# Sixteen key and value pieces of layer 1 moved from the convolution's stage into layer 0's cross attention, and routing counts in bf16

## The chip, the cores and the metric

The kernel runs on one core of a Trainium2 chip. The metric is the device time of one execution in microseconds. Engines: PE is the matrix engine, PEld its weight loads, DVE the vector engine, ACT the scalar engine, POOL GpSimd, SP the queue that issues most transfers. A `q` behind an engine's name is its sequencer.

## The reference

A decoder of two layers over x of 32 x 128 x 256 (32 tiles of 128 rows), all f32. Each of six stages is followed by a residual sum and a layer norm:

```python
x = ln(x + L0_attn(x))                      # 16 heads, correlation scores
x = ln(x + L0_xattn(x, ctx, ctx))           # 16 heads of 16, |i - j| <= 64
x = ln(x + L0_ffn(x))                       # rms norm, 8 bit rounding, one matmul
x = ln(x + L1_attn(x))                      # long convolution (EMA), gated attention
x = ln(x + L1_xattn(x, ctx, ctx))           # 16 heads of 64
x = ln(x + L1_ffn(x))                       # 8 experts, top 2, capacity, gelu
# L1_xattn begins with, for every tile of ctx:
k = ctx @ Wk.T + bk; v = ctx @ Wv.T + bv    # 256 -> 1024 each
# L1_ffn: pos = cumsum(onehot(top_i)) over the 4096 rows, keep = pos < capacity
```

Layer 1's keys and values depend on ctx alone, so they can be made at any time before layer 1's cross attention.

## The kernel before

**Keys and values in pieces.** `EarlyKeysValues` (L1248) makes them ahead, for 16 groups of two tiles, 8 pieces a group, 128 pieces in all: four of keys (two banks' halves, each with its bias on ACT) and four of values. `make` puts the matmuls of a piece on PE, `keep` its copy on ACT; PSUM banks alternate (`self.ps[n % 2]`), and `make` of piece n waits until piece n - 2 is kept. ACT also issues the stores to DRAM (keys of a group when its first value piece is kept, values when the next group's first key piece is kept, 1 MB each) and the load of the context of the group after next. `load_weights` brings 1 MB of key weights, the bias and 1 MB of value weights; the contexts of groups 0 and 1 are loaded behind them on SP. The first piece waits for the key weights, the bias and the first context.

**Where the pieces go.** Before: 4 at the end of layer 0's cross attention, 66 in the feed-forward stage (9 + 8 x 6 + 9), 58 in the convolution's stage: 20 ahead of the convolution (`CONV_FIRST`), one behind each of its 16 steps, 22 after it.

**Layer 0's cross attention** (`l0_xattn`, L794) works on 8 groups of 4 tiles. Every engine walks the same list of steps s in its own written order (`walk`, L866), each entry (lag, count, function) acting on tile s - lag. Per tile: PE makes the scores; DVE takes their maximum, subtracts it (`shift`, in two halves), later sums the exponentials (`sums`); ACT makes the exponentials; POOL scales them; PE transposes them (`transpose_e`, four parts), two steps later, multiplies by the values (`apply`), and one step later by the output weights (`multiply`); DVE adds the residual. `transpose_e` of a tile's second part waits for the residual, as they share a bank. Per group, in the four steps before its first tile: the transposes of x (part 0), the projections of q (part 1), k (part 2) and v (part 3), all through the two banks `ps_p`, which the early pieces share. ACT copies each of them out (`copy_xt`, `bias_q`, `bias_k`, `copy_v`). The step of part 0 is the step in which a group's first tile is scored (s % 4 = 0). On SP, `load(g)` brings x and the context of a group; the context's buffer is free when the values of group g - 2 are projected, and SP issues in order.

**The feed-forward stage** (`l0_ffn`) puts its pieces by number after `L0X_LAST`.

**The convolution's stage** (`mega_conv`, L1664): SP issues four loads of the normalised x in runs of 256 bytes, then the weights of the gated attention. PE makes the first pieces, waits for the input, then runs 16 steps of the convolution with a piece behind each, then the rest. When ACT has written the last step's result, SP issues four stores of it, also in runs of 256 bytes, waits for them and issues the first loads of it for the gated attention. The next stage begins when all engines are done, ACT's stores too.

**Layer 1's cross attention** (`l1_xattn`, L2123) counts rows per expert in groups of two tiles: `count` multiplies `hot` (128 x 32, zeros and ones) once by a triangle of ones (`upto`) and once by ones, both f32; DVE adds up the counts.

## Time and profile before

| what | us |
|---|---|
| runs of the kernel before | 2377.5, 2382.82, 2383.73; median 2382.82 |
| profiled execution, its own time | 2379.42 |
| its span in the trace | 2377.7 |
| PE busy | 2168.2 (91%) |
| DVE busy | 1329.3 (56%) |
| ACT busy | 1111.6 (47%) |
| POOL busy | 923.3 (39%) |
| mean granted PE clock, share of full speed | 0.967 |

The stages follow one another: layer 0's attention to about 404 us, its cross attention to 726, the feed-forward stage to 871, the convolution's stage 872 to 1005, the gated attention to about 1305, layer 1's cross attention to 1817, the experts to the end. A share over the whole span mixes these, so the windows and timelines by stage say more. Busy of PE includes the latency of the last matmul of a run, so a PE that is shown busy all the time can still hold gaps of a tenth of a microsecond.

### The profile page before, as it was taken

The page shows a single profiled execution, that of the slowest core. Times are in us where ns is not written, and L with a number is a line of the kernel's source. Part 1 is how long each engine was busy: PE and PEld are TensorE (multiplying, and loading weights), DVE is VectorE, ACT ScalarE, POOL GpSimd, SP SyncE. Part 2 cuts the span into 40 slices and gives each one's busy share as a digit, 9 for nine tenths or more (in the row PEclk, how much of TensorE's full clock was granted, in tenths as well). Part 3 has the DMA queues.
Part 4 walks back from the last instruction along what each step waited for, and adds up shares of the span by engine and source line. Part 5 has one row for each costly group of instructions (what it writes and reads, how often), then busy time and mean ns, then how long its engine had stood idle before and what let it go on. Part 6 is the DMA issues. An engine that isn't in the chain of part 4 may idle for free. (4 is left out here: it accounts for less than half of the span.)

```text
span 2377.7 us, 44258 instructions
## 1 busy us (share of the span) xinstructions
PE 2168.2 (91%) x16874; PEld 1732.3 (73%) x16874; DVE 1329.3 (56%) x2519; ACT 1111.6 (47%) x1915; POOL 923.3 (39%) x946
## 2 busy tenths in 40 slices
PE   6899896889978999999999899999995999999993
PEld 5788775566655667667676688888874888888893
DVE  6899894899984910045546478887783111111113
ACT  3788784676765645443342455555552111111113
POOL 4788774445553940001101244444452222222222
PEclk8999997999999999999999899999997999999997
DMA  5445653111204786631211323333324756666564
GB/s 149 114 119 139 167 143 91 37 37 37 72 19 170 250 259 205 223 107 36 71 36 45 129 89 109 109 115 114 104 86 175 245 178 178 181 188 191 185 208 153
DMA packets 198465, 312.93 MB, mean 132 GB/s; under 512 B 63729, under 2 KB 174961, under 8 KB 184945
## 3 DMA queue, kind: packets, MB, share of 16 engines
q1 hardware_dynamic: 178192, 254.99, 33.8%
q0 software_dynamic: 13440, 17.90, 4.2%
q10 hardware_dynamic: 6624, 37.23, 4.0%
q8 instruction: 136, 2.23, 0.4%
q14 instruction: 73, 0.59, 0.1%
HBM read 188.62 MB, written 121.45 MB: 130 GB/s over the span
## 5 line engine op out<-in xcount | busy, mean ns | idle before, releaser
L2804 ACT ACTIVATE dec_area<-me_ps_h 128x512 f32<-128x512 f32 (+1 forms) x160 | 88.7, 555 | 424.0 <-PE me_ps_h L2782 414.8
L2845 DVE TENSOR_SCALAR me_yo<-me_ps_y,moe_xg 128x256 f32<-128x256 f32 x72 | 34.8, 484 | 428.1 <-PE me_ps_y L2792 399.6
L2713 POOL DMA_INDIRECT xo<-me_yo,me_row x72 | 112.8, 1567 | 410.8 <-DVE me_yo L2845 337.1
L2247 POOL TENSOR_TENSOR l1x_e<-l1x_e,l1x_ri 128x1024 f32<-128x1024 f32 x64 | 121.8, 1903 | 239.3 <-DVE l1x_ri L2507 239.3
L2782 PE MATMUL me_ps_h<-me_xt,me_w 128*128 128x256 f32 (+1 forms) x1056 | 210.0, 357 | 0.0
L2792 PE MATMUL me_ps_y<-me_w,dec_area 128*128 128x256 f32 x944 | 209.2, 379 | 0.7 <-DVE me_yo L2845 0.7
L2792 PEld LDWEIGHTS me_ps_y<-me_w,dec_area 128*128 128x128 f32 x944 | 178.7, 190 | 25.1 <-issue 1.1
L2782 PEld LDWEIGHTS me_ps_h<-me_xt,me_w 128*128 128x128 f32 x1056 | 181.7, 190 | 20.2
L908 POOL TENSOR_TENSOR l0x_e<-l0x_e,l0x_ri 128x1024 f32<-128x1024 f32 x64 | 120.1, 1898 | 151.0 <-DVE l0x_ri L1155 151.0
L2346 PE MATMUL l1x_ps_p<-l1x_xct,dec_area 128*128 128x256 f32 x512 | 125.0, 389 | 0.7 <-ACT l1x_xct L2432 0.7
L2445 ACT ACTIVATE l1x_e<-l1x_sx 128x1024 f32<-128x1024 f32 x64 | 67.4, 1054 | 116.4 <-DVE l1x_sx L2498 116.2
L2384 PE MATMUL l1x_ps_o<-dec_area,l1x_ot 128*128 128x256 f32 x512 | 118.7, 385 | 1.4 <-ACT l1x_ot L2455 1.4
L2384 PEld LDWEIGHTS l1x_ps_o<-dec_area,l1x_ot 128*128 128x128 f32 x512 | 94.7, 190 | 15.2 <-ACT l1x_ot L2455 1.7
L2504 DVE TENSOR_REDUCE l1x_rs<-l1x_e 128x8 f32<-128x1024 f32 x64 | 78.0, 1219 | 49.5 <-ACT l1x_e L2445 47.1
L2346 PEld LDWEIGHTS l1x_ps_p<-l1x_xct,dec_area 128*128 128x128 f32 x512 | 94.4, 194 | 13.9 <-ACT l1x_xct L2432 1.1
L2495 DVE TENSOR_REDUCE l1x_top<-l1x_ps_s 128x8 f32<-128x1024 f32 x64 | 77.6, 1212 | 45.9 <-PE l1x_ps_s L2357 45.4
L1836 POOL TENSOR_TENSOR ma_ve<-ma_mv,ma_eps 128x2 f32<-128x2 f32 x16 | 6.4, 399 | 226.2 <-DVE ma_mv L2003 226.2
L1028 PE MATMUL l0x_ps_e<-dec_ident,l0x_e 128*128 128x128 f32 x512 | 73.9, 278 | 21.4 <-DVE l0x_r L1166 15.4
L486 POOL TENSOR_SCALAR_AFFINE_SELECT l0ah_c<-l0ah_c 128x1024 f32<-128x1024 f32 x64 | 70.0, 1093 | 59.9 <-DVE l0ah_c L584 59.7
L2450 ACT ACTIVATE l1x_et<-l1x_ps_e 128x512 f32<-128x512 f32 x128 | 72.8, 595 | 35.2 <-PE l1x_ps_e L2365 34.7
L1028 PEld LDWEIGHTS l0x_ps_e<-dec_ident,l0x_e 128*128 128x128 f32 x512 | 58.8, 142 | 41.0 <-issue 23.7
L1143 DVE TENSOR_REDUCE l0x_top<-l0x_ps_s 128x8 f32<-128x1024 f32 x64 | 77.3, 1208 | 18.1 <-PE l0x_ps_s L1012 17.9
(426 smaller groups left out, 5381.6 us busy)
## 6 DMA issues: line engine op xcount, KB each, us to landing
me_w<-in_w SPq DMA_DIRECT2D x33, 2048.0 KB, 9.2
xs<-dec_zero SPq DMA_DIRECT2D x31, 1032.0 KB, 6.6
k<-kv_kt ACTq DMA_DIRECT2D x16, 1024.0 KB, 4.8
v<-kv_va ACTq DMA_DIRECT2D x16, 1024.0 KB, 4.6
l1x_kt<-k SPq DMA_DIRECT2D x16, 1024.0 KB, 5.0
l1x_va<-v SPq DMA_DIRECT2D x16, 1024.0 KB
moe_w_first<-in_w SPq DMA_DIRECT2D x7, 2048.0 KB, 9.6
moe_xg<-xs SPq DMA_DIRECT2D x32, 258.0 KB, 2.9
```

Source lines behind the costliest of these rows:

```text
L908: pool.tensor_tensor(e[:, n % 2, u, :, :], e[:, n % 2, u, :, :], spread(ri[:, n % 2, u, :], P), ALU.mult).then_inc(e_scaled, 1)
L1028: last = pe.transpose(ps_e[j % 2][:, i, :], e[:, n % 2, j // 2, 4 * (j % 2) + i, :], ident[:, :])
L1143: dve.tensor_reduce(top[:, u, :], scores, AX.X, ALU.max).then_inc(maxed, 1)
L2247: pool.tensor_tensor(e[:, n % 2, u, :, :], e[:, n % 2, u, :, :], spread(ri[:, n % 2, u, :], P), ALU.mult).then_inc(e_scaled, 1)
L2346: last = pe.matmul(ps_p[i % 2][:, c * GP:(c + 1) * GP], w_q[:, k, at], xct[:, k, :], start=k == 0, stop=k == 1)
L2384: last = pe.matmul(ps_o[:, 0:2, :].rearrange("p a b -> p (a b)"), ot[:, c, :], w_o[:, c, :], start=c == 0, stop=c == C - 1)
L2495: dve.tensor_reduce(top[:, u, :], scores, AX.X, ALU.max).then_inc(maxed, 1)
L2504: dve.tensor_reduce(rs[:, n % 2, u, :], e[:, n % 2, u, :, :], AX.X, ALU.add).then_inc(summed, 1)
L2713: pool.indirect_dma_start(token_rows, bass.IndirectOffsetOnAxis(row[:, j % 2, q:q + 1], 0), yo[:, j % 2, q, :], None, compute_op=ALU.add). ...
L2782: last = pe.matmul(ps_h[i % HB][:, f % 2, 0:P * size(j)], weights(j)[:, FFN * c + f * P:FFN * c + f * P + P], xt[:, j % 2, c, 0:P * size(j ...
L2792: last = pe.matmul(ps_y[q][:, 0:D], h[:, j % 2, f, q * P:(q + 1) * P], weights(j)[:, W2 + D * f:W2 + D * f + D], start=f == 0, stop=f == F ...
L2804: act.activation(h[:, j % 2, 2 * i:2 * i + 2, 0:P * size(j)], ps_h[i % HB][:, :, 0:P * size(j)], ACT.Gelu).then_inc(gelued, 1)
```

## The change

It changes the place of 16 pieces. In layer 0's cross attention each group's first step (s % 4 = 0) gets two pieces, one behind the v projection's slot and one behind the score, before `apply`; 4 more remain at the end. The transposes of x for the next group move from ahead of the q projection's slot to the end of the step, and ACT's `copy_xt` from this step to the start of the next. The transposes wait for the kept pieces and the pieces for the copied values, since all use the same two banks. The weights and the first contexts are issued on SP behind `load(2)`, where they were issued in the sixth round of SP's loop over groups. In the convolution's stage 13 pieces stand ahead, 16 among and 13 behind. The routing counts' operands are bf16.

```diff
-L0X_LAST, FFN_FIRST, FFN_STEP, FFN_LAST = 4, 9, 6, 9
+L0X_STEPS, L0X_LAST, FFN_FIRST, FFN_STEP, FFN_LAST = 2 * TILES // 4, 4, 9, 6, 9
+L0X_PIECES = L0X_STEPS + L0X_LAST
...
                 load(1)
                 load(2)
+                kv.load_weights(sp)
+                for early in range(2):
+                    kv.load_ctx(sp, early)
                 for g in range(NG):
                     if g + 3 < NG:
                         load(g + 3)
-                    if g + 3 == NG:
-                        kv.load_weights(sp)
-                        for early in range(2):
-                            kv.load_ctx(sp, early)
...
-                        slot_free(pe, v_copied, 2 * g + i, 2)
+                        if g:
+                            item_done(pe, kv.kept, 2 * (g - 1) + i)
...
                 def early(n):
-                    if n == 0:
-                        pe.wait_ge(v_copied, 2 * NG)
-                    kv.make(pe, n, n + 1)
-                walk([(2, TILES, lambda n: transpose_e(n, (0, 1))), at_part(0, transposes), at_part(1, project_q), at_part(2, project_k),
-                      at_part(3, project_v), (2, TILES, lambda n: transpose_e(n, (2, 3))), (0, TILES, score), (2, TILES, apply), (3, TILES, multiply),
-                      (TILES + 1, L0X_LAST, early)])
+                    kv.make(pe, L0X_STEPS + n, L0X_STEPS + n + 1)
+
+                def among(g, i):
+                    item_done(pe, v_copied, 2 * g + i)
+                    kv.make(pe, 2 * g + i, 2 * g + i + 1)
+
+                def at_group(i):
+                    return (0, TILES, lambda n: among(n // G, i) if n % G == 0 else None)
+                walk([(2, TILES, lambda n: transpose_e(n, (0, 1))), at_part(1, project_q), at_part(2, project_k),
+                      at_part(3, project_v), at_group(0), (2, TILES, lambda n: transpose_e(n, (2, 3))), (0, TILES, score), at_group(1),
+                      (2, TILES, apply), (3, TILES, multiply), at_part(0, transposes), (TILES + 1, L0X_LAST, early)])
...
-                walk([(2, TILES, lambda n: copy_et(n, (0, 1))), (8, TILES, normalise), (1, TILES, lambda n: exponentials(n, 1)),
-                      (2, TILES, lambda n: copy_et(n, (2, 3))), (2, TILES, copy_ot), at_part(0, copy_xt), (-G, 1, spread_bias), at_part(1, bias_q), at_part(2, bias_k), at_part(3, copy_v), (-2, 1, band_constants),
-                      (0, TILES, lambda n: exponentials(n, 0)), (TILES + 1, 2, lambda n: kv.keep(act, n, n + 1)),
+                walk([at_part(1, copy_xt), (-G, 1, spread_bias), (2, TILES, lambda n: copy_et(n, (0, 1))), (8, TILES, normalise), (1, TILES, lambda n: exponentials(n, 1)), keep(0),
+                      (2, TILES, lambda n: copy_et(n, (2, 3))), keep(1), (2, TILES, copy_ot), at_part(1, bias_q), at_part(2, bias_k), at_part(3, copy_v), (-2, 1, band_constants),
+                      (0, TILES, lambda n: exponentials(n, 0)), (TILES + 1, 2, lambda n: kv.keep(act, L0X_STEPS + n, L0X_STEPS + n + 1)),
...
-CONV_FIRST, CONV_PIECES = 20, 1
+CONV_FIRST, CONV_PIECES = 13, 1
...
-        ones, upto = kit.sb("ones", [P, P]), kit.sb("upto", [P, P])
+        ones, upto = kit.sb("ones", [P, P], BF16), kit.sb("upto", [P, P], BF16)
...
-        hot = kit.sb("hot", [P, TOPK, G, EXPERTS])
+        hot = kit.sb("hot", [P, TOPK, G, EXPERTS], BF16)
```

## Rows read from the trace of the kernel before

**Rows 1.** Windows: PE, PEld, DVE, ACT, POOL busy, granted clock, DMA share, GB/s.
```profile
540.00:600.00 60.00, 55.03 (x556) 39.72 (x559) 55.41 (x73) 43.41 (x72) 30.85 (x23) 1.00 0.17 54
```

**Rows 2.** Timeline, a q projection's step: start, us, engine, line, idle before.
```profile
569.12 3.60 PE L973 MATMUL l0x_ps_p<-l0x_xt,dec_area 128*128 128x512 f32 x8
...
573.52 1.15 PE L1005 MATMUL l0x_ps_s<-l0x_kt,l0x_qt 32*128 32x256 f32 x16
...
574.95 1.23 DVE L1143 TENSOR_REDUCE l0x_top<-l0x_ps_s 128x8 f32<-128x1024 f32 x1 [0.69 <-PE l0x_ps_s L1012]
```

**Rows 3.** Timeline, the step with s % 4 = 0 and the next one's start.
```profile
595.89 0.41 DVE L1166 TENSOR_TENSOR l0x_r<-l0x_ps_e,l0x_xb 128x256 f32<-128x256 f32 x1
...
596.91 1.04 PE L958 MATMUL l0x_ps_p<-dec_ident,l0x_x 128*128 128x128 f32 x8
...
601.54 1.08 PE L1037 MATMUL l0x_ps_e<-l0x_et,l0x_va 128*32 128x128 f32 x32 [0.54 <-ACT l0x_et L1112]
...
602.55 1.13 PE L1049 MATMUL l0x_ps_e<-dec_area,l0x_ot 128*128 128x256 f32 x4
...
602.97 1.08 ACT L1086 ACTIVATE l0x_xt<-l0x_ps_p 128x512 f32<-128x512 f32 x2
...
604.33 0.41 DVE L1166 TENSOR_TENSOR l0x_r<-l0x_ps_e,l0x_xb 128x256 f32<-128x256 f32 x1
604.51 1.06 ACT L1106 ACTIVATE l0x_e<-l0x_sx 128x1024 f32<-128x1024 f32 x1 [0.46 <-DVE l0x_sx L1146]
...
605.36 1.02 PE L973 MATMUL l0x_ps_p<-l0x_xt,dec_area 128*128 128x512 f32 x2
```

**Rows 4.** Timeline, eight pieces behind the convolution.
```profile
972.42 7.07 PE L1310 MATMUL mc_ps_kv<-kv_ct,kv_w_kv 128*128 128x256 f32 x32
...
979.33 7.03 PE L1317 MATMUL mc_ps_kv<-kv_w_kv,kv_ct 128*128 128x512 f32 x16
```

**Rows 5.** Timeline of SP and PE, and a DMA row (count, KB each, us to landing).
```profile
420.09 0.33 SPq L931 DMA_DIRECT2D l0x_cxt<-in_ctx  x1
...
421.33 1.15 PE L1005 MATMUL l0x_ps_s<-l0x_kt,l0x_qt 32*128 32x256 f32 x16
...
627.49 2.16 SPq L1287 DMA_DIRECT2D kv_w_kv<-in_ywk  x1
...
630.76 0.96 SPq L1293 DMA_DIRECT2D kv_ct<-in_ctx  x2
...
kv_ct<-in_ctx SPq DMA_DIRECT2D x2, 256.0 KB, 7.8
```

**Rows 6.** A window and the timeline where PE starts after a gap.
```profile
729.00:730.00 1.00, 0.00 (x0) 0.01 (x1) 0.00 (x0) 0.00 (x0) 0.16 (x1) 0.50 0.00 0
...
730.03 9.42 PE L1317 MATMUL ffn_ps_kv<-kv_w_kv,kv_ct 128*128 128x512 f32 x16 [5.39 <-PEq L85]
```

**Rows 7.** The convolution's input by tile (queue us), and its first matmul.
```profile
L1202 SPq DMA_DIRECT2D cv_xg<-xn x4: 705/4676/7546, 872.0 to 882.2; - x4
...
DMA to landing us min/median/max: 7.4/16.4/20.6
...
906.52 1.92 PE L1708 MATMUL mc_ps<-cv_xg,cv_t 128*128 128x128 f32 x8
```

**Rows 8.** Timeline behind the convolution: output, reload, next stage.
```profile
961.66 21.82 SPq L1685 DMA_DIRECT2D mx<-cv_xg  x4
...
993.11 14.76 SPq L1245 DMA_DIRECT2D mw_xin<-mx  x8
...
1005.46 3.87 PE L2025 MATMUL ma_ps_t<-dec_ident,mw_xin 128*128 128x128 f32 x16 [5.33 <-PEq L85]
```

**Rows 9.** Timeline of a count on PE, and bf16 weight loads (ns min/median/max).
```profile
1467.45 0.31 PE L2415 MATMUL l1x_ps_p<-l1x_hot,l1x_upto 128*128 128x32 f32 x2
...
1467.91 1.16 PE L2357 MATMUL l1x_ps_s<-l1x_kt,l1x_qt 64*128 64x128 f32 x16
...
L1568 PEld LDWEIGHTS ffn_ps_t<-dec_identb,ffn_xq x64: 97/98/98, 752.2 to 841.7; 128*128 128x128 bf16 x64
```

More of the change, by code:

```diff
@@ L1124, in normalise, with keep @@
                                    bias=ln[:, g % 2, 1, t:t + 1]).then_inc(normed, 1)
-                walk([(2, TILES, lambda n: copy_et(n, (0, 1))), (8, TILES, normalise), (1, TILES, lambda n: exponentials(n, 1)),
-                      (2, TILES, lambda n: copy_et(n, (2, 3))), (2, TILES, copy_ot), at_part(0, copy_xt), (-G, 1, spread_bias), at_part(1, bias_q), at_part(2, bias_k), at_part(3, copy_v), (-2, 1, band_constants),
-                      (0, TILES, lambda n: exponentials(n, 0)), (TILES + 1, 2, lambda n: kv.keep(act, n, n + 1)),
-                      (TILES + 5, L0X_LAST - 2, lambda n: kv.keep(act, n + 2, n + 3))])
+                def keep(i):
+                    return (0, TILES, lambda n: kv.keep(act, 2 * (n // G) + i, 2 * (n // G) + i + 1) if n % G == 0 else None)
+                walk([at_part(1, copy_xt), (-G, 1, spread_bias), (2, TILES, lambda n: copy_et(n, (0, 1))), (8, TILES, normalise), (1, TILES, lambda n: exponentials(n, 1)), keep(0),
+                      (2, TILES, lambda n: copy_et(n, (2, 3))), keep(1), (2, TILES, copy_ot), at_part(1, bias_q), at_part(2, bias_k), at_part(3, copy_v), (-2, 1, band_constants),
+                      (0, TILES, lambda n: exponentials(n, 0)), (TILES + 1, 2, lambda n: kv.keep(act, L0X_STEPS + n, L0X_STEPS + n + 1)),
+                      (TILES + 5, L0X_LAST - 2, lambda n: kv.keep(act, L0X_STEPS + n + 2, L0X_STEPS + n + 3))])
             @block.vector
@@ L1539, in apply @@
                                        bias=ln[:, g % 2, 1, t:t + 1]).then_inc(normed, 1)
-                kv.keep(act, L0X_LAST, L0X_LAST + 2)
+                kv.keep(act, L0X_PIECES, L0X_PIECES + 2)
                 sum_squares(0)
@@ L1543, in _ @@
                 act.activation(w[:, :, :], w_i[:, :, :], ACT.Copy).then_inc(w_ready, 1)
-                kv.keep(act, L0X_LAST + 2, L0X_LAST + 5)
+                kv.keep(act, L0X_PIECES + 2, L0X_PIECES + 5)
                 sum_squares(1)
-                kv.keep(act, L0X_LAST + 5, L0X_LAST + FFN_FIRST)
+                kv.keep(act, L0X_PIECES + 5, L0X_PIECES + FFN_FIRST)
                 for s in range(1, NG + 2):
-                    first = L0X_LAST + FFN_FIRST + FFN_STEP * (s - 1)
+                    first = L0X_PIECES + FFN_FIRST + FFN_STEP * (s - 1)
                     if 0 <= s - 1 < NG:
@@ L1578, in multiply @@
                             last.then_inc(multiplied, 1)
-                kv.make(pe, L0X_LAST, L0X_LAST + FFN_FIRST)
+                kv.make(pe, L0X_PIECES, L0X_PIECES + FFN_FIRST)
                 pe.wait_ge(w_ready, 1)
                 for s in range(NG):
-                    first = L0X_LAST + FFN_FIRST + FFN_STEP * s
+                    first = L0X_PIECES + FFN_FIRST + FFN_STEP * s
                     transposes(s)
@@ L1673, in mega_conv @@
         convolved, activated, stored = (kit.sem(n) for n in ("convolved", "activated", "stored"))
-        begin = L0X_LAST + FFN_FIRST + FFN_STEP * TILES // 4 + FFN_LAST
+        begin = L0X_PIECES + FFN_FIRST + FFN_STEP * TILES // 4 + FFN_LAST
         among = begin + CONV_FIRST
```

## The prediction

> **What bounds the kernel now.** I read first the windows, because a mean over the whole span mixes stages with different limits [rows 1]. In layer 0's cross attention (about 421 to 725 us) DVE is busy 55.4 of 60 us and PE 55.0 of 60: two engines are nearly full, and the reader should look for who waits for whom. That is in the timelines, which I read next at each place that the change touches.
>
> In the cross attention of layer 0 a step with a projection goes like this [rows 2]: the eight matmuls of the projection start at 569.12, the score at 573.52, and DVE starts its maximum at 574.95 after 0.69 idle, released by PE. So in the three projection steps of a group of four PE sets the pace. The fourth step holds only the small transposes of the next group, about 0.9 us from 596.91 [rows 3], and PE waits 0.54 for ACT's copy before `apply` at 601.54. DVE's residuals are at 595.89 and 604.33, 8.44 us apart, with DVE the busy one. This is the only step with room on PE, and the 16 pieces go there. From one group's q projection to the next's it is 36.2 us (569.12 to 605.36).
>
> The convolution's stage is PE matmuls and pieces end to end [rows 7, 8], with two transfers beside them: its input, and its output with the reload.
>
> **Price of a piece.** Four pieces of keys start at 972.42 and the next ones at 979.33: 6.9 us for four, 1.72 us each [rows 4]. Sixteen are 27.5 us of PE at full clock, taken out of one stage and put into another. The question is what each stage pays or gets.
>
> **Edit 1, two pieces in each group's first step (paid).** I walk the step through, with the times of rows 3 as the old positions. Piece one takes the place of the transposes at 596.91 and ends 598.63. The second half of `transpose_e` takes 0.97 (569.12 to 573.52 less a projection, which has the eight entries of two value pieces, 3.43), the score 1.42 (573.52 to 574.94): score done 601.02. DVE reaches it near 602 (its subtraction, reduction and residual before 604.33 take 2.4), so piece one is free. Piece two: 601.02 to 602.74. `apply` (1.01: 601.54 to 602.55) starts 602.74 instead of 601.54, `multiply` follows at 603.75 and is done, with its 0.2 of latency, at 604.92. DVE's residual stood at 604.33: 0.6 late. Next on PE come the moved transposes (0.88), to 605.60, then 0.94 of `transpose_e`, and the q projection. It needs `copy_xt`, which used to run at 602.97, well ahead. Now it stands at the start of ACT's next step, behind the exponential of 604.51 to 605.57, and takes 1.08 + 0.1: the projection starts about 606.75, not 605.36. That is 1.4 us late, the step after is set by PE, so DVE waits for all of it. Queued behind `copy_xt` on ACT are the `et` copies and the rest of that step; PE wants those only 3.4 us later, after the projection.
>
> Six groups (1 to 6) pay 1.4: 8.4. The last group has no projection behind it and pays about half a microsecond. Bounds: 0 per group if PE's idle takes both pieces (the 8.44 step is then unchanged), and 3.44 if no idle can be used. I take 1.4, which is what is left of 3.44 after the idle around the step.
>
> **Edit 2, loading the weights at the start (paid).** SP is a queue in order: `load(2)` holds its context part until `v_projected`, so it issues at 420.09 [rows 5]. The 2 MB of weights and both contexts come behind it. Before, the same five issues began at 627.49, the first context was issued at 630.76, and a context landed 7.8 us after its issue: 11.1 us from first issue to landing. From 420.45 this gives 431.5. The first piece is ahead of the first score in PE's program, and that score stood at 421.33. Nothing covers this: the pipeline is empty, so DVE, ACT and POOL wait as well. Delay 10.2 us, plus the piece itself, 1.7, plus the clock: after a gap of 5.39 us, with PEclk at 0.50, 16 matmuls took 9.42 us against 7.03 us [rows 4, 6], 2.4 us lost. The score would be done near 437 instead of 422.75, 14.3 later. In the next steps piece two, the transposes, `copy_xt` and the q projection stand in line (+2.3), and the start-up, in which no engine is full yet, gives about that much back by tile 3 (an estimate). I take 14, between 11 (landing at 430, no loss by the clock) and 18.
>
> The Trainium skill, "TensorE: Matmul & The Clock Gate", section "What's actually happening", says that the throttled clock is the default and that activity releases it. The trace agrees (0.50 after the gap in rows 6). Without that rule and row this delay would be 11.6, with it 14; both gaps that the change opens pay for it, so it speaks against the change.
>
> Other movements: the four stores of finished groups and the loads of two contexts on ACT's queue now run within the cross attention, where DMA is nearly idle (its share is 0.17 of the engines in the first window of rows 1); I cost them at nothing, at worst 0.3 us of ACT issue each. The numbering shift leaves the feed-forward stage with the same pieces in the same phase of eight (4 and 20, both the first values of a group): 0.
>
> **Edit 3, seven pieces fewer ahead of the convolution (gained).** 20 pieces end with the first convolution matmul at 906.52; 13 would end 12 us sooner, near 894.4. But the convolution also needs its input: the last of the four loads was issued at 882.2 and the longest landing is 20.6 us, so it is there at 902.8 [rows 7]. In the new order the store of keys that follows the sixteenth piece no longer shares the engines with it; I allow 1.7 and say 901. So PE idles 6.6 us, falls to the low clock and loses 2.3. Gain 906.5 - 901 - 2.3 = 3. Bounds: 1 (input at 902.8 and full loss) and 12 (input not in the way).
>
> **Edit 4, nine pieces fewer behind it (gained).** The output is issued from 961.66, and the reload of it from 993.11, when the last store has landed: 31.4 us [rows 8]. The next stage starts at 1005.46, because 22 pieces and their last store run until just before. With 13 pieces (22.4 us and some 5 of store) PE and ACT are done 28 us after 961.66, and the transfer chain is late next: 31.4, four issues 2.6, the barrier 0.8: 34.9 instead of 43.8. Gain 8.9. Both orders have four stores of 1 MB beside the output, so I leave 31.4. Bounds: 5 (the reload is slower or its data is waited for) and 10.
>
> **Edit 5, counts in bf16 (gained).** A count is four f32 matmul entries that hold PE from 1467.45 to 1467.91, 0.45 us, with no idle before the score that follows it, so PE's time is the stage's here [rows 9]. In bf16 I expect two entries. The nearest row is the 128x128 bf16 transposes, whose weights load in 0.098; two of those bound the new cost by 0.2 from above. I take 0.15 and a gain of 0.3 for each of 16 groups: 4.8. Bounds 0 (the count not split in two entries, or waited for) and 6. The DVE writes of `hot` have 16 or 32 elements, too small for type to matter.
>
> **Sum.** +8.4 + 0.5 + 14 - 3 - 8.9 - 4.8 = +6.2 us. The profiled execution took 2379.42 us around a span of 2377.7, so the sum gives 2385.6. That execution lies 3.4 below the median 2382.82; the mean of the four times known is 2380.9, and from there I predict 2387. What a measurement can tell from no change is 0.3%, 7.1 us: the forecast is slower, just inside it.
>
> **The rivals.**
> A, no stall at the start: the weights land before the first score would have run (decided at 422; it needs an issue at about 411). Then -14: 2373, faster. For it: on paper nothing but the order on SP holds the loads back. Against: that order does, with the issue at 420.09.
> B, PE's idle takes both pieces: per group 0. 2387 - 8.9 = 2378, no change; with a quicker input load ahead of the convolution (up to -9 more) faster. For it: the two engines are each idle 4.6 to 5 of 60 us [rows 1]. Against: `copy_xt`, now behind the exponential.
> C, no idle can be used: the group pays both pieces, 3.44, in seven groups, since the loop residual, projection, score, residual leaves no room: 24.1 for 8.9, +15: 2402, slower. Against: PE's 0.54 wait in that step and DVE's place ahead of it.
> D, the output chain grows: stores now fall in the same 31 us, and the gain behind the convolution is 3 instead of 8.9: 2393.
> E, the bf16 count saves nothing: 2392.
>
> **Chances.** Forecast 0.50, own range 2381 to 2393, of it 0.27 within 0.3% and 0.23 slower. A 0.10, faster. B 0.17: 0.12 same, 0.05 faster. C 0.10, D 0.08, E 0.05: slower but for 0.03. Together faster 0.15, same 0.42, slower 0.43. The range takes in B and D and the edges between A and C: 2376 to 2398.
>
> **What would show it.** The first score near 435 and PE empty from 420 to 431 with PEclk 0.5 after. The q projection right behind `copy_xt` and DVE's idle before L1143 at the first score of each projection run about 1.6 instead of 0.7; q projections of two groups 37.6 us apart instead of 36.2. The convolution's first matmul about 29 us after its stage begins at 872.0 (34.5 before), with PE idle ahead of it. From the output's first issue to the next stage 35 us instead of 44. Counts 0.15 us on PE. A first piece that doesn't wait, or q projections still 36.2 apart, would make the prediction wrong.

## The result: 13.6 us slower, and the profile after

The changed kernel takes 2392.36 us (median, 2386.34 to 2398.73), the kernel before, on the same chip, 2377.57 us (2373.05 to 2383.73). The ratio of all runs is 1.0057 with an interval of 1.0045 to 1.0070: slower by 13.6 us, by 10.7 at least and 16.6 at most (the two medians alone are 14.8 apart; below I go by the ratio). The forecast was 2387 and slower, 6.2 us above the 2380.9 that the kernel before was taken to need. Its direction held and its size was half of what came. The profiled execution has a span of 2392.2 us (2377.7 before).

The window in the middle of layer 0's cross attention answers [rows 1]. Its columns are the same.

```profile
568.00:628.00 60.00, 58.02 (x610) 43.14 (x609) 54.00 (x72) 43.37 (x76) 31.33 (x23) 1.00 0.22 72
```

PE has gone from 55.0 to 58.0 of 60 us and DVE from 55.4 to 54.0: where two engines were nearly full, PE alone sets the pace now.

The start of that stage, against [rows 5] (timeline of the changed kernel: start, us, engine, line, operation, idle before):

```profile
423.37 0.33 SPq L932 DMA_DIRECT2D l0x_cxt<-in_ctx  x1
423.74 0.44 SPq L1295 DMA_DIRECT2D kv_w_kv<-in_ywk  x1
...
433.81 3.75 PE L1318 MATMUL l0x_ps_p<-kv_ct,kv_w_kv 128*128 128x256 f32 x8 [10.47 <-DMA kv_ct<-in_ctx]
437.49 1.15 PE L1006 MATMUL l0x_ps_s<-l0x_kt,l0x_qt 32*128 32x256 f32 x16
...
438.93 1.22 DVE L1151 TENSOR_REDUCE l0x_top<-l0x_ps_s 128x8 f32<-128x1024 f32 x1 [18.58 <-PE l0x_ps_s L1013]
```

SP could issue the weights only behind the context part at 423.37. PE stood idle for 10.47 us, and its first piece then took 3.75 us instead of 1.9. The stage itself began 3.4 us later than in the trace of before (407.55, not 404.15), in code that is the same in both. In the twelve traces of the experiments this start lies between 401.8 and 412.5, so I count each stage from its own beginning. From the stage's start to DVE's first maximum it is 31.4 us (18.6 before).

The fourth step of a group, against [rows 3]:

```profile
587.13 1.99 PE L1318 MATMUL l0x_ps_p<-kv_ct,kv_w_kv 128*128 128x256 f32 x8
589.05 1.08 PE L1038 MATMUL l0x_ps_e<-l0x_et,l0x_va 128*32 128x128 f32 x32
590.06 1.13 PE L1050 MATMUL l0x_ps_e<-dec_area,l0x_ot 128*128 128x256 f32 x4
591.03 1.04 PE L959 MATMUL l0x_ps_p<-dec_ident,l0x_x 128*128 128x128 f32 x8
591.90 1.04 PE L1029 MATMUL l0x_ps_e<-dec_ident,l0x_e 128*128 128x128 f32 x8
592.87 2.41 PE L974 MATMUL l0x_ps_p<-l0x_xt,dec_area 128*128 128x512 f32 x5
...
591.73 1.09 ACT L1092 ACTIVATE l0x_xt<-l0x_ps_p 128x512 f32<-128x512 f32 x2
592.87 0.30 PEld L974 LDWEIGHTS l0x_ps_p<-l0x_xt,dec_area 128*128 128x128 f32 x2 [0.16 <-ACT l0x_xt L1092]
...
591.23 0.42 DVE L1174 TENSOR_TENSOR l0x_r<-l0x_ps_e,l0x_xb 128x256 f32<-128x256 f32 x1 [0.71 <-PE l0x_ps_e L1050]
...
598.80 1.23 DVE L1151 TENSOR_REDUCE l0x_top<-l0x_ps_s 128x8 f32<-128x1024 f32 x1 [1.39 <-PE l0x_ps_s L1013]
```

PE's matmuls run through the whole step without a gap, and only the first weights of the q projection wait 0.16 for ACT's copy, which ends at 592.82. DVE's residual waits 0.71 for PE, and its next maximum 1.39 (0.69 in [rows 2]). The q projections follow one another in 37.73 to 37.75 us (36.24 before).

The convolution's stage, against [rows 7, 8]; the third row is the convolution's first matmul:

```profile
896.46 20.19 SPq L1210 DMA_DIRECT2D cv_xg<-xn  x4
...
927.95 2.06 PE L1716 MATMUL mc_ps<-cv_xg,cv_t 128*128 128x128 f32 x8 [8.83 <-DMA cv_xg<-xn]
...
984.47 22.27 SPq L1693 DMA_DIRECT2D mx<-cv_xg  x4
1019.48 5.92 SPq L1253 DMA_DIRECT2D mw_xin<-mx  x8
...
1023.89 3.90 PE L2033 MATMUL ma_ps_t<-dec_ident,mw_xin 128*128 128x128 f32 x16 [16.45 <-DMA mw_xin<-mx]
```

And the counts in layer 1's cross attention, against [rows 9] (busy us, mean ns of one, idle before):

```profile
L2423 PE MATMUL l1x_ps_p<-l1x_hot,l1x_upto 128*128 128x32 bf16 x15 | 2.7, 181 | 3.7 <-DVE l1x_hot L2549 3.7
L2424 PE MATMUL l1x_ps_p<-l1x_hot,l1x_ones 128*128 128x32 bf16 x15 | 2.7, 177 | 0.0
```

```profile
1457.40 0.18 PE L2423 MATMUL l1x_ps_p<-l1x_hot,l1x_upto 128*128 128x32 bf16 x1
...
1457.67 1.16 PE L2365 MATMUL l1x_ps_s<-l1x_kt,l1x_qt 64*128 64x128 f32 x16
```

Each part is one matmul now, not two. The pair holds PE for 0.27 us, from 1457.40 to the score at 1457.67 (0.46 from 1467.45 to 1467.91 in [rows 9]), so a count gives back 0.19 us here and not 0.3.

The account, from the two traces, each stretch from its own beginning:

| stretch | before | after | difference | forecast |
|---|---|---|---|---|
| cross attention of layer 0, start to last maximum | 299.0 | 323.2 | +24.2 | +22.9 |
| convolution: stage start to first matmul | 34.5 | 31.5 | -3.0 | -5.5 |
| convolution: first matmul to output's issue | 55.1 | 56.5 | +1.4 | +2.3 |
| output's issue to reload's issue | 31.4 | 35.0 | +3.6 | 0 |
| reload's issue to next stage's first matmul | 12.4 | 4.4 | -7.9 | -8.9 |
| cross attention of layer 1 | 508.0 | 505.4 | -2.6 | -4.8 |

The -2.6 of the last row hides a difference that is not the change's: the first count stands 97.8 us into that stage (96.2 before), at a granted clock of 0.94 in this stretch (0.95 before), and what follows it is 4.2 shorter. The rest of the difference in span is the upstream 3.4, a feed-forward stretch that happened to be 3.2 longer in the trace of before (168.8 from the last maximum to the convolution's stage; 165.6 to 166.1 in three other traces with the same code there), and differences below 1. The stage of the convolution gave 6.0 of the hoped-for 11.9.

### The profile page after: what moved, and what is told of

Same layout as the page of the kernel before. It is cut to its first block and busy times, and to the rows that moved or that the text cites. A ratio compares the mean times of both kernels' runs of the same rounds, so it can differ in the third digit from the quotient of the medians.

```text
span 2392.2 us, 44206 instructions
## 1 busy us (share of the span) xinstructions
PE 2168.4 (91%) x16842; PEld 1728.6 (72%) x16842; DVE 1329.8 (56%) x2519; ACT 1112.3 (46%) x1915; POOL 922.3 (39%) x946
## 5 line engine op out<-in xcount | busy, mean ns | idle before, releaser
L2853 DVE TENSOR_SCALAR me_yo<-me_ps_y,moe_xg 128x256 f32<-128x256 f32 x72 | 34.8, 484 | 429.1 <-PE me_ps_y L2800 410.1
L2354 PEld LDWEIGHTS l1x_ps_p<-l1x_xct,dec_area 128*128 128x128 f32 x512 | 95.7, 196 | 14.8 <-ACT l1x_xct L2440 1.6
L2458 ACT ACTIVATE l1x_et<-l1x_ps_e 128x512 f32<-128x512 f32 x128 | 72.8, 596 | 32.5 <-PE l1x_ps_e L2373 31.9
L585 DVE SCALAR_TENSOR_TENSOR l0ah_c<-l0ah_f,l0ah_ps_s 128x1024 f32<-128x1024 f32 x64 | 77.6, 1213 | 17.4 <-ACT l0ah_f L771 17.4
```

The lines of the kernel that those rows point to most:

```text
L585: dve.scalar_tensor_tensor(out=c[:, n % 2, u, :, :].rearrange("p (r g) k -> p r g k", g=2), in0=f[:, u, :, :].rearrange("p (r g) k -> p r ...
L2354: last = pe.matmul(ps_p[i % 2][:, c * GP:(c + 1) * GP], w_q[:, k, at], xct[:, k, :], start=k == 0, stop=k == 1)
```

## The experiments

Where an experiment builds on another, its diff is against that one. All ratios are to the kernel before on the same chip; the traces are one for each kernel.

**1. The weights first.**

```
+                kv.load_weights(sp)
+                for early in range(2):
+                    kv.load_ctx(sp, early)
                 load(1)
                 load(2)
-                kv.load_weights(sp)
-                for early in range(2):
-                    kv.load_ctx(sp, early)
```

> The changed kernel with one edit: SP issues layer 1's key and value weights and the first two contexts before the loads of groups 1 and 2, not behind the context part of group 2 (which waits for the first group's value projection). My theory: of the +13.6 us of the change about 14.7 are the stall at the start of layer 0's cross attention (first key context waited for 10.5 us by PE, low clock after), and it is only SP's order that makes it. The issues then begin at the stage's start, the contexts land 11 to 12 us later, before the first score, and 11 to 14 us come back: 2378 to 2381 us, 0 to +4 against the kernel before. PE's wait for the first context disappears, tile 3's maximum starts 45 to 48 us after the stage's first instruction (58.8 in the changed kernel, 44.2 before). Rival: the start is set by the two pieces and the moved transposes in PE's order; then only 3 to 5 us come back (2388).

Measured: 2376.05 us, ratio 0.9986 (0.9977 to 0.9995). The one move of five issues on SP's queue turns the change from slower to a little faster: 1.0057 to 0.9986, 17 us. That is more than the 11 to 14 expected, and 3.4 us below the kernel before where 0 to 4 above it was expected.

```profile
407.00 0.38 SPq L1295 DMA_DIRECT2D kv_w_kv<-in_ywk  x1
...
423.18 1.89 PE L1318 MATMUL l0x_ps_p<-kv_ct,kv_w_kv 128*128 128x256 f32 x8
425.00 1.15 PE L1006 MATMUL l0x_ps_s<-l0x_kt,l0x_qt 32*128 32x256 f32 x16
```

The first piece waits for nothing and runs at full clock; tile 3's maximum starts 45.15 us into the stage (58.8 in the changed kernel, 44.2 before). From stage start to last maximum it is 309.6 us, so 13.7 of the 24.2 were the stall. The pieces-in-order rival is out. In the other kernels below "weights first" means this edit.

**2. One piece per group.** Eight pieces instead of sixteen, 17 ahead of the convolution and 17 behind it, weights first.

```
-L0X_STEPS, ... = 2 * TILES // 4, ...
+L0X_STEPS, ... = TILES // 4, ...
...
-                    kv.make(pe, 2 * g + i, 2 * g + i + 1)
+                    kv.make(pe, g, g + 1)
...
-CONV_FIRST, CONV_PIECES = 13, 1
+CONV_FIRST, CONV_PIECES = 17, 1
```

> The changed kernel with the weights first on SP as in the other experiment, and one piece per group in the cross attention instead of two (8 instead of 16; ahead of the convolution 17, beside it 16, behind it 17). My theory, as forecast: the first piece of a group is hidden in PE's idle time and the second pays 1.5 us; then the q projections of two groups stand 36.2 to 36.5 us apart (36.3 before, 37.7 in the changed kernel). Ahead of the convolution the input sets the time (first matmul 31 to 32 us after the stage begins) with PE never idle, behind it 17 pieces and their last store take 37 to 38. Sum against before: 0 for the groups, 2 for the start, -3 and -6 at the convolution, -2.6 for the counts: 2368. Rival: every piece costs alike, 0.75 each, 36.9 to 37.0 us apart: 2373.

Measured: 2375.59 us, ratio 0.9976 (0.9962 to 0.9989). Both expectations failed: the q projections stand 37.58 us apart, 1.34 more than before and only 0.15 less than with two pieces. So half of the pieces costs nearly all of the price. The timeline of a fourth step says why:

```profile
613.72 0.41 DVE L1174 TENSOR_TENSOR l0x_r<-l0x_ps_e,l0x_xb 128x256 f32<-128x256 f32 x1
...
613.90 1.06 ACT L1112 ACTIVATE l0x_e<-l0x_sx 128x1024 f32<-128x1024 f32 x1 [0.95 <-DVE l0x_sx L1154]
614.86 1.07 ACT L1092 ACTIVATE l0x_xt<-l0x_ps_p 128x512 f32<-128x512 f32 x2
...
615.98 2.41 PE L974 MATMUL l0x_ps_p<-l0x_xt,dec_area 128*128 128x512 f32 x5 [0.68 <-ACT l0x_xt L1092]
```

DVE's residual is not late, so the piece looks hidden; but ACT copies the transposed input only after the exponential, and PE waits for it. This points at the order and not at the piece; experiments 5 and 6 test it.

**3. The bf16 counts alone, on the kernel before.**

```
-        ones, upto = kit.sb("ones", [P, P]), kit.sb("upto", [P, P])
+        ones, upto = kit.sb("ones", [P, P], BF16), kit.sb("upto", [P, P], BF16)
-        hot = kit.sb("hot", [P, TOPK, G, EXPERTS])
+        hot = kit.sb("hot", [P, TOPK, G, EXPERTS], BF16)
```

> The kernel before with one edit: the routing's ones, upper triangle and one-hot tiles in bf16. By the forecast a count falls from 0.45 to 0.15 us of PE and 16 groups give back 4.8 us: 2373. By the trace of the changed kernel layer 1's cross attention was 2.6 us shorter, with a first q projection that was 1.2 longer at the low clock: between 2.6 and 4: 2374 to 2375. Rival: the counts stand beside other work and give nothing: 2377.6.

Measured: 2373.22 us, ratio 0.9975 (0.9964 to 0.9987): 5.9 us faster, 3.1 at least. The stage took 503.2 us against 508.0 in the trace of before, the forecast's 4.8. Over all traces it is 508.0 to 510.5 with f32 (three) and 502.9 to 505.4 with bf16 (eleven). The changed kernel's 505.4 is the longest of its kind, which makes its own -2.6 too small a figure for this edit. But the 4.8 don't come as 16 times 0.3. From one group's count to the next's it is 29.24 us eleven times in a row before and 29.04 here (once 29.14), 0.2 less each; the last two groups, in which PE idles ahead of the count, give another 2. The last count, before and in this kernel (the granted clock is 0.50 in both):

```profile
1805.32 0.64 PE L2415 MATMUL l1x_ps_p<-l1x_hot,l1x_upto 128*128 128x32 f32 x2 [2.62 <-DVE l1x_hot L2541]
1805.77 0.61 PE L2416 MATMUL l1x_ps_p<-l1x_hot,l1x_ones 128*128 128x32 f32 x2
```

```profile
1796.64 0.21 PE L2415 MATMUL l1x_ps_p<-l1x_hot,l1x_upto 128*128 128x32 bf16 x1 [2.62 <-DVE l1x_hot L2541]
1796.68 0.19 PE L2416 MATMUL l1x_ps_p<-l1x_hot,l1x_ones 128*128 128x32 bf16 x1
```

**4. Seventeen ahead of the convolution.** The changed kernel with 17 and 9.

```
-CONV_FIRST, CONV_PIECES = 13, 1
+CONV_FIRST, CONV_PIECES = 17, 1
```

> The changed kernel with 17 pieces ahead of the convolution and 9 behind it instead of 13 and 13. The changed kernel idles 8.8 us ahead of the convolution for its input, and from the output's issue to its reload it takes 35.0 us where it was 31.4 before. My theory: the four pieces fill the idle time (first convolution matmul still 31 to 32 us after the stage begins, no low clock after it, -1.4), and with fewer pieces behind the output's issue, three 1 MB stores stand beside it instead of four, so that chain goes back to 31 to 32: together -4 to -5 against the changed kernel, 2388. Rival: the chain's 35 has nothing to do with the stores of keys and values; then it stays 35 and the gain is 1.4: 2391. Second rival: the extra store ahead of the convolution delays its input by 2 to 3 us and eats the gain: 2392 or more.

Measured: 2385.03 us, ratio 1.0027 (1.0016 to 1.0037), 7 us better than the change's 1.0057 and more than the 4 to 5 expected; in the traces the convolution's stage is 4.1 shorter (127.4 to 123.3). The first convolution matmul came 31.0 us into the stage with 1.49 us of idle time: the input sets this time, and four more pieces fit in front of it for nothing. The chain from output to reload is 31.3, as the first theory had it. The low clock stayed, against the theory: the 7 us after the gap show 0.76, and the convolution's loop took 56.5 us, as in the changed kernel.

**5. The order by itself.** The kernel before, no piece moved; only the transposes go behind `multiply` on PE and their copy behind the exponential on ACT.

```
-                walk([(2, TILES, lambda n: transpose_e(n, (0, 1))), at_part(0, transposes), ...
+                walk([(2, TILES, lambda n: transpose_e(n, (0, 1))), ...
-                      ... (2, TILES, apply), (3, TILES, multiply),
+                      ... (2, TILES, apply), (3, TILES, multiply), at_part(0, transposes),
-                walk([(2, TILES, lambda n: copy_et(n, (0, 1))), ... (2, TILES, copy_ot), at_part(0, copy_xt), ...
+                walk([at_part(1, copy_xt), (2, TILES, lambda n: copy_et(n, (0, 1))), ... (2, TILES, copy_ot), ...
```

> The kernel before, with all pieces where they were, and only the order of the fourth step changed as the change has it: the next group's transposes behind multiply on PE, their copy behind the exponential on ACT. It prices the order by itself. By my forecast's walk the first piece is hidden and the second pays 0.6 us of the 1.4, the copy behind the exponential the other 0.8: so 0.8 per group, spacing 37.0, +5 us (2384). By the one-piece run, in which PE waited for the copy and DVE's residual was not late, it is 1.3 per group, spacing 37.5, +8 to +9 us (2387). Rival: without a piece the idle time takes it: spacing 36.2, 2379.

Measured: 2387.93 us, ratio 1.0033 (1.0020 to 1.0046), 7.9 us slower, and the q projections 37.57 us apart: the second expectation. The wait is in the open here:

```profile
615.84 0.41 DVE L1166 TENSOR_TENSOR l0x_r<-l0x_ps_e,l0x_xb 128x256 f32<-128x256 f32 x1
615.90 1.13 PE L1028 MATMUL l0x_ps_e<-dec_ident,l0x_e 128*128 128x128 f32 x8
616.02 1.06 ACT L1106 ACTIVATE l0x_e<-l0x_sx 128x1024 f32<-128x1024 f32 x1 [1.44 <-DVE l0x_sx L1146]
...
616.98 1.07 ACT L1086 ACTIVATE l0x_xt<-l0x_ps_p 128x512 f32<-128x512 f32 x2
...
618.10 2.41 PE L973 MATMUL l0x_ps_p<-l0x_xt,dec_area 128*128 128x512 f32 x5 [1.07 <-ACT l0x_xt L1086]
```

**6. One piece, transposes early.** The one-piece kernel with the transposes between the score and `apply`, and their copy ahead of the output copy.

```
-                      (0, TILES, score), (2, TILES, apply), (3, TILES, multiply), at_part(0, transposes),
+                      (0, TILES, score), at_part(0, transposes), (2, TILES, apply), (3, TILES, multiply),
-                walk([at_part(1, copy_xt), ...
+                walk([..., (2, TILES, lambda n: copy_et(n, (2, 3))), at_part(0, copy_xt), (2, TILES, copy_ot), ...
```

> The kernel of the one-piece experiment with the order of the fourth step restored: the next group's transposes on PE stand between the score and apply (where PE idled 0.94 us), no longer behind multiply, and ACT copies them ahead of the output copy and the exponential. With one piece per group the q projections stood 37.6 us apart and PE waited 0.68 us for that copy, which stood behind the exponential, while DVE's residual was not late. Theory: the 1.3 us per group are the order's price, not the piece's; the spacing returns to 36.2 to 36.4, six groups give back 7 to 8 us: 2368. Rival: the piece's 1.7 us on PE are the price, and the spacing stays at 37.3 or more: 2375.

Measured: 2366.87 us, ratio 0.9947 (0.9930 to 0.9965), as expected. The spacing is 36.23 to 36.25 us in the later groups, that of the kernel with no pieces there, and the stage takes 298.5 us to its last maximum (299.0 before).

```profile
597.37 1.88 PE L1325 MATMUL l0x_ps_p<-kv_w_kv,kv_ct 128*128 128x512 f32 x4
...
601.48 1.09 PE L959 MATMUL l0x_ps_p<-dec_ident,l0x_x 128*128 128x128 f32 x8
602.50 1.08 PE L1038 MATMUL l0x_ps_e<-l0x_et,l0x_va 128*32 128x128 f32 x32
...
605.82 1.45 PE L974 MATMUL l0x_ps_p<-l0x_xt,dec_area 128*128 128x512 f32 x3
```

The transposes fill the gap in which PE had waited for ACT before `apply`, and the q projection follows its transposes without a wait. Eight pieces are made here for nothing.

**7. Two pieces, transposes early.** Weights first, the same two moves with both pieces.

```
-                      ... (0, TILES, score), at_group(1), (2, TILES, apply), (3, TILES, multiply), at_part(0, transposes), ...
+                      ... (0, TILES, score), at_group(1), at_part(0, transposes), (2, TILES, apply), (3, TILES, multiply), ...
...
-                walk([at_part(1, copy_xt), ... keep(1), (2, TILES, copy_ot), ...
+                walk([... keep(1), at_part(0, copy_xt), (2, TILES, copy_ot), ...
```

> The changed kernel with the weights first on SP and two pieces per group, but with the next group's transposes between the second piece and apply, and their copy on ACT ahead of the output copy: the order that took away the whole price with one piece per group (37.6 to 36.2 us apart). Theory: with two pieces PE has no idle left in that step (3.44 us of pieces against about 2 of idle), so the order no longer matters and the second piece pays by itself: spacing 37.5 to 37.8, 2376 to 2378. Rival: the copy behind the exponential was the whole price here too: spacing 36.3 to 36.6, 2368.

Measured: 2384.18 us, ratio 1.0014 (1.0004 to 1.0025), spacing 38.4 to 38.6 where 37.5 to 37.8 and 2376 to 2378 us were expected. The rival is dead, and the theory is 0.6 to 1.1 us a group short: with a second piece the order matters the other way. What stands before `apply` delays the residual, which waits 2.30 us for PE here and 0.71 in the changed kernel. Beyond that the chain behind the convolution is 36.2 us here (34.3 in the weights-first kernel).

```profile
581.29 0.66 PE L959 MATMUL l0x_ps_p<-dec_ident,l0x_x 128*128 128x128 f32 x4 [0.49 <-ACT kv_kt L1351]
581.87 1.08 PE L1038 MATMUL l0x_ps_e<-l0x_et,l0x_va 128*32 128x128 f32 x32
...
584.05 0.42 DVE L1174 TENSOR_TENSOR l0x_r<-l0x_ps_e,l0x_xb 128x256 f32<-128x256 f32 x1 [2.30 <-PE l0x_ps_e L1050]
```

So the price of a group is 0 with one piece in this order, 1.34 with one in the change's order, 1.33 with none in that order, 1.49 with two in it and 2.1 to 2.4 with two in this one.

**8. Eighteen ahead, eight behind.** Weights first, `CONV_FIRST` 18 instead of 13.

> The changed kernel with the weights first on SP, and 18 pieces ahead of the convolution and 8 behind it. 18 pieces end when the input lands (31 us after the stage begins), so PE doesn't idle and the clock doesn't fall (-1.4 to -1.8), and behind the convolution three stores stand beside the output instead of four (-3): 31.3 for the chain. Against the weights-first kernel -4 to -5: 2371. Rival: the stores in the first 31 us delay the input, front 33 to 34, and the gain is 2 at most: 2374.

Measured: 2373.21 us, ratio 0.9976 (0.9965 to 0.9988), 2.4 us better than the weights-first kernel by the ratios (4 to 5 expected; in the traces the convolution's stage is 4.9 shorter, 127.0 to 122.1). PE meets the input without an idle row, 31.1 us into the stage; the loop is 55.2 us, so the clock is kept; the chain is 31.3.

**9. Eleven ahead, fifteen behind.** Weights first, `CONV_FIRST` 11.

> The changed kernel with the weights first on SP, and 11 pieces ahead of the convolution and 15 behind it instead of 13 and 13. From the output's first issue to its reload it took 31.3 to 31.9 us in three traces and 34.3 to 35.0 in three others; the former have three 1 MB stores of keys and values issued in the first 24 us of it, the latter four. With 15 pieces behind, the fourth store is issued 27 us after the output. Theory: the chain falls to 31.5 although PE has two pieces more behind it; the input still sets the front (31.2), so against the weights-first kernel -3: 2373. Rival: the chain depends on the number of pieces or of bytes, and stays at 34 to 35: 2376 or more.

Measured: 2383.79 us, ratio 1.0016 (1.0006 to 1.0026). The expectation failed: the chain is 37.1 us. I had counted the stores wrong; one goes out 0.7 us after the output and four follow. The front is 31.1 once more, with 11.93 us of idle time before it. The kernel is 7 us slower than the weights-first one by the ratios, of which its stage shows 2.7 in the traces (127.0 to 129.8).

**10. The last store held.** Weights first; ACT's last copy of values and the store behind it wait for the convolution's output to land.

```
-                kv.keep(act, among + CONV_PIECES * CH // 4, kv.COUNT)
+                kv.keep(act, among + CONV_PIECES * CH // 4, kv.COUNT - 1)
+                act.wait_ge(stored, 16 * G)
+                kv.keep(act, kv.COUNT - 1, kv.COUNT)
```

> The changed kernel with the weights first on SP, and ACT's last copy of layer 1's values, with the 1 MB store behind it, held back until the convolution's output has landed (its order among the pieces stays). In the weights-first kernel that store is issued 23.6 us after the output's first issue, took 10.4 us to land in the changed kernel, and the output's last part landed at 34.3 to 34.9. Theory: it is this store, of all that runs there, that costs the 3.5 us; without it the chain from first issue to reload is 31.3 to 31.9, and the stage ends with the held store, some 37 us after the first issue instead of 38.8: -1.5 against the weights-first kernel, 2375. Rival: the earlier stores or fewer pieces make the chain long; it stays at 34 to 35 and the held store adds to it, the stage ends at 40: 2378.

Measured: 2376.50 us, ratio 0.9987 (0.9978 to 0.9996), the same as without the wait where 1.5 us less was expected. But the chain did what the theory says, 970.00 to 1001.60, 31.6 us instead of 34.3:

```profile
1001.61 0.60 ACT L1360 ACTIVATE kv_va<-mc_ps_kv 128x512 f32<-128x512 f32 x1 [9.71 <-DMA mx<-cv_xg]
1002.23 0.34 ACTq L1337 DMA_DIRECT2D v<-kv_va  x1
```

The held store then runs beside the reload: the next stage starts 38.1 us after the output's issue instead of 38.8. That store costs the chain 2.7 us between these two traces (the chain of unchanged stores was 34.3 to 36.2 in three), and moving it only moves the cost.

**11. Sixteen ahead, eighteen behind.** The transposes-early kernel, `CONV_FIRST` 16.

> The kernel of the transposes-early experiment (one piece per group, weights first) with 16 pieces ahead of the convolution and 18 behind it instead of 17 and 17. The fall of the chain with 15 pieces behind did not come (37.1 us): there a first store went out 0.7 us after the output and a fifth 27.1 us after it. What the seven traces so far have in common is the time of a store against the output's end: chains of 31.3 to 31.9 where the fourth store is issued 26.5 us after the output's first issue or there is none, 34.3 to 35.8 where it is issued at 23.6 to 24.8. With 18 pieces behind, stores fall at 5.8, 12.7, 19.6, 26.5 and 32.2. Theory: the chain falls from 35.8 to 31.5 although one piece more stands behind it; the stage then ends with its last store, 37 us after the output's first issue instead of 40.5; ahead of the convolution PE idles 3 us and the clock costs 1.3: about -2 against the transposes-early kernel, 2365. Rival: the chain depends on the number of pieces behind, and stays at 35 or more: 2368.

Measured: 2364.44 us, ratio 0.9928 (0.9914 to 0.9942), the fastest kernel of this study; its interval overlaps that of the transposes-early kernel (0.9930 to 0.9965). The time came as expected, the mechanism did not: the chain is 35.4 us, not 31.5. The convolution's stage took 126.7 us in all (126.5 in the transposes-early kernel), so the two are equal by the traces.

**12. Twenty-four ahead, on the kernel before.** `CONV_FIRST` 24 instead of 20.

> The kernel before with one number changed: 24 pieces ahead of the convolution and 18 behind it instead of 20 and 22; cross attention and counts as they were. In the sixteen-eighteen kernel the stores stood at the same times after the output's first issue as in the kernel before (5.8, 12.7, 19.6, 26.5), with keys and values exchanged, and the chain to the reload took 35.4 us, not 31.5. So what holds it to 31.5 in three traces with 22 pieces behind is either which pieces those are, or something else of the kernel before. Theory 1, which pieces: here they are the same 18 as in the sixteen-eighteen kernel, so 35 to 35.5; the front is 6.9 us longer, the stage ends some 40 us after the output's first issue instead of 43.8: +3, 2384. Theory 2, the rest of the kernel: the chain stays at 31.4 to 31.9, the stage ends with the last store after 37: about 0, 2381.

Measured: 2381.59 us, ratio 0.9992 (0.9981 to 1.0004): no change. The convolution's stage is 2.5 us longer in the trace (136.0 for 133.5), and the chain is 33.0 us, between the two theories. The largest landing time of an output part is the last row of the view by tile, here of the changed kernel and of the held one:

```profile
DMA to landing us min/median/max: 2.4/2.6/21.1
```

```profile
DMA to landing us min/median/max: 2.5/2.7/19.0
```

All chains, with the stores of keys and values (1 MB each) that are issued before the chain ends, by their issue after the output's:

| kernel | stores issued at, us | chain, us |
|---|---|---|
| before, bf16 only, order only | 5.8, 12.7, 19.6, 26.5 | 31.4, 31.9, 31.5 |
| before with 24 ahead | 5.8, 12.7, 19.6, 26.5, 32.2 | 33.0 |
| sixteen and eighteen | 5.8, 12.7, 19.6, 26.5, 32.2 | 35.4 |
| changed, weights first, two pieces early | 4.1, 11.0, 17.9, 23.6 | 35.0, 34.3, 36.2 |
| one piece, one piece early | 4.1, 11.0, 17.9, 24.8, 30.5 | 34.8, 35.8 |
| eleven | 0.7, 7.6, 14.4, 21.3, 27.1 | 37.1 |
| seventeen | 4.1, 11.0, 16.8 | 31.3 |
| eighteen | 2.4, 9.3, 15.0 | 31.3 |
| last store held | 4.1, 11.0, 17.9 | 31.6 |

With three stores issued in the first 30 us it is 31.3 to 31.6 each time, with four 31.4 to 36.2, with five 37.1.

## Why the prediction was right in direction and half in size

**The weights at the start.** Right: PE's wait (10.47 us for a walk of 10.2), the slow piece after it, the first score done 31.4 us into the stage (the forecast's 437 lay 32.9 after the start in the trace of before), 14 us forecast in all and 13.7 by experiment 1. The piece after the gap took 3.75 us, in experiment 1 the same piece took 1.89; the granted clock was 0.50 while it ran in the changed kernel (0.68 in the 10 us from 431) and 1.00 in experiment 1. The Trainium skill, "TensorE: Matmul & The Clock Gate", section "What's actually happening", says that the throttled state is the default; the trace agrees (0.50 after the idle time).

**Two pieces per group.** The size was right (1.4 forecast, 1.49 measured), and so was the walk that gave it: it has PE free for the q projection at 606.54 (605.60 and 0.94 of `transpose_e`) and the copy done at 606.75, two limits 0.2 apart of which the later one counts. In the changed kernel they are as close: the projection starts at 592.87, when PE is free, and its first weights wait 0.16 for the copy. Experiment 5 shows that the copy's limit alone costs 1.33 with no piece at all, and one piece adds nothing to it, as the walk had it ("piece one is free"). What was wrong is the reason put beside the walk, that 1.4 is "what is left of 3.44 after the idle". With one piece, half of those 3.44 us, the price falls only to 1.34; so it is not the pieces' time less the idle time. My expectation for experiment 5 misread the walk in the same way when it split the 1.4 into 0.6 and 0.8. Rival B (both pieces hidden) and C (nothing hidden) are both out. That the price is avoidable, with one piece and the transposes left before `apply`, no rival said.

**Ahead of the convolution.** The step that I put as "I allow 1.7" for a store that no longer shares the engines failed: in the changed kernel the input landed 31.4 us into the stage, no sooner than in [rows 7] (30.8). With four stores in that stretch (16 to 18 pieces ahead) the first matmul came at 30.8 to 31.1, with three (11 and 13 ahead) at 31.1 to 31.5, once at 32.5 (experiment 10). So that store does not set the landing. The low clock cost 1.4, not 2.3. Front and clock together gave 1.7 us instead of 3.

**Behind the convolution.** This is the term that was mis-sized: 4.4 us for 8.9. The half that I named came (reload to next stage -7.9), but "both orders have four stores, so I leave 31.4" did not hold: the chain grew by 3.6 us. The number of stores was right. Their times were not: the fourth is issued 23.6 us after the output, 26.5 in the kernel before. Experiment 10 shows that this store is worth 2.7 of the chain; the kernels with three stores agree (31.3). A second, smaller part was left out: the next stage's first matmul waits for the reload's data (its row names the transfer `mw_xin<-mx`) and starts 4.4 us behind the reload's issue where 3.4 were put down. Together that is rival D, which had been given 0.08 and the price of 5.9: 4.5 came. The trace of the changed kernel shows how unlike the two transfers are in the 35 us of the chain, the output on q1 and the stores on q10 (packets, MB, share of the 16 DMA engines):

```profile
DMA packets 17024, 8.39 MB, mean 239 GB/s; under 512 B 16512, under 2 KB 16512, under 8 KB 16512
...
q1 hardware_dynamic: 16448, 4.19, 48.4%
q10 hardware_dynamic: 576, 4.19, 32.7%
```

In this trace 205 GB/s are moved while the output is alone, up to 390 while a store is beside it. The Trainium skill, "DMA: Bandwidth & Descriptors", section "Queues, rings and completion order", says that a DMA engine takes turns between the queues it has work for, a packet of several descriptors at a time. No trace here shows the turns; that the output loses by them is argued, not shown.

**The counts.** The sum came out right (4.8 forecast, 4.8 between the traces and 5.9, 3.1 to 8.6, by the measured times of experiment 3), the price of one count did not: PE is held 0.27 us by it, not 0.15, and gets back 0.2 of the 0.3. What made up for it are the last groups, where PE waits for DVE before the count and the whole of the pair's 1.06 us, 0.23 in bf16, stands in the open. That the two errors cancel is luck. Rival E is out.

**The sum.** +24.2 - 3.0 + 1.4 + 3.6 - 7.9 makes +18.3. With the counts at -4.8 (two traces) to -5.9 (the measured times) it is +12.4 to +13.5, and +13.6 (10.7 to 16.6) was measured. Of the 7.4 us that the forecast of +6.2 missed, 4.5 stand behind the convolution (3.6 the chain, 1.0 the wait for the reload's data, each rounded), 1.3 are the front and its clock, 1.3 the cross attention. That 2387 lies within 5.4 us of the measured 2392.36 is in part luck: it was built on 2380.9 for the kernel before, which took 2377.57 in the comparison. Rival A was wrong for this kernel and right for the one it points at: issued first, the weights do land in time.

**What stays open.** Why four stores cost the chain nothing in three traces, 1.6 us in one and 3.9 in another with the same issue times. Neither which pieces they are (experiment 12 against 11) nor the rest of the kernel explains it alone. The same stores as in the changed kernel gave 34.3, 35.0 and 36.2, so about 2 us of such a difference need no cause in the order of stores. And the 17 us that experiment 1 gave back are 3 more than the stall in its trace; the two intervals (some 3 us on the change's side, 2 on the other) are wide enough for that. They are not for experiment 9, measured on another chip: it is 7 us slower than experiment 1 by the ratios and 2.7 by the stage that the edit touches. No run says where the rest is.

## What to carry to other kernels

Work moved into an engine's idle time was cheap here only where the instructions around it kept their places: the first piece was free, and the transposes moved behind `multiply`, with their copy queued behind an exponential, cost 1.33 us a group. Look at each transfer that the moved work needs, in its queue's order, and issue it before anything in that queue that waits. And a stage gives back only what stands outside its chain of transfers when its engines do less: nine pieces fewer behind the output, 15 us of PE, gave 4.4. The stores that follow the work come earlier and may fall into that very chain.

## What the runs showed of the hardware

- The granted clock after idle time of PE ahead of the convolution, and the length of its loop (55.1 to 55.2 us with no gap), one trace each: the clock is a mean over the next 7 us of the two levels, 1.00 being 2.4 GHz and 0.50 being 1.2 GHz.

| idle us | granted clock in the next 7 us | loop us |
|---|---|---|
| 1.26, 1.28 | 1.00, 1.00 | 55.2, 55.2 |
| 1.49 | 0.76 | 56.5 |
| 2.93 | 0.78 | 55.9 |
| 8.58, 8.71, 8.83 | 0.57, 0.76, 0.68 | 56.9, 56.0, 56.5 |
| 9.84, 11.93 | 0.74, 0.57 | 56.1, 57.0 |

The gap of 1.49 us cost as much as the one of 8.83, and gaps of like length differ by up to 1 us.
- A count of 32 columns against 128x128 weights is four PE entries in f32 and two in bf16; it held PE for 0.46 and 0.27 us where the next matmul followed at once.
- The same code upstream ended between 401.8 and 412.5 us in the fourteen traces. Two profiled executions can differ by this alone, which is nearly the size of the change; stages have to be compared each from its own start.
- A 1 MB store took 3.8 us to land when the engines were free, and 5.4 to 11.1 beside the convolution's output; 10.4 to 11.1 in the three traces that issue it 23.6 us after the output's first issue.
